# A graph network's finishing stages: bias and shift added on GpSimd, the norm's end writes the new rows, and the norm's root as exp(-0.5 ln)

## What is computed

```python
h = jax.nn.elu(layer_norm(x @ w_in + b_in, g_in, bt_in))
for i in range(L):
    identity = h
    y = gat_conv(h, src, dst, w_l[i], a_s[i], a_d[i], b_l[i])
    y = jax.nn.elu(y)
    y = layer_norm(y, g_l[i], bt_l[i])
    h = y + identity
```

```python
def layer_norm(x, g, b):
    mu = jnp.mean(x, axis=-1, keepdims=True)
    var = jnp.var(x, axis=-1, keepdims=True)
    return (x - mu) * jax.lax.rsqrt(var + EPS) * g + b
```

## Time and profile before

| | us |
|---|---|
| median of 3 runs | 6753.14 |
| lowest, highest | 6741.82, 6756.97 |
| the profiled execution | 6749.72 |
| its span (first to last instruction) | 6747.9 |

### The profile page before, as it was taken

The page is one execution under the profiler, slowest core; times in us unless marked ns, Lnnn a source line. Parts: engine busy times, 40 slices in busy tenths (PEclk is TensorE's granted clock), DMA queues, the critical chain, the costliest instruction groups (busy, mean ns, idle before and its releaser), DMA issues. The chain is left out here.

```text
span 6747.9 us, 97821 instructions
## 1 busy us (share of the span) xinstructions
PE 5290.4 (78%) x22256; PEld 3728.3 (55%) x22256; DVE 4764.2 (71%) x13068; ACT 3945.6 (58%) x13294; POOL 3528.1 (52%) x3571
## 2 busy tenths in 40 slices
PE   1758888845788888458888878999989787777798
PEld 1634445424455555335555547888874566565446
DVE  5756666685677777847777768888871587777793
ACT  4558888874788888648888874444436322111142
POOL 3377777717777776277777740000000577777501
PEclk8878888876899999669999988999999898888899
DMA  6355555435444444454444435555557534333402
GB/s 185 115 151 137 144 140 143 132 103 156 122 124 124 123 128 108 125 144 122 124 126 124 123 82 189 189 190 195 191 189 268 175 117 125 109 108 101 124 2 78
DMA packets 511899, 919.90 MB, mean 136 GB/s; under 512 B 89659, under 2 KB 345611, under 8 KB 511435
## 3 DMA queue, kind: packets, MB, share of 16 engines
q0 software_dynamic: 166320, 446.82, 24.5%
q1 hardware_dynamic: 345259, 469.88, 21.4%
HBM read 773.29 MB, written 152.30 MB: 137 GB/s over the span
## 5 line engine op out<-in xcount | busy, mean ns | idle before, releaser
L1826 POOL DMA_INDIRECT gm_got<-scratch_feat,keep_src_tab x2490 | 2386.6, 958 | 778.5 <-issue 675.0
L2048 ACT ACTIVATE gm_got<-gm_got 128x64 f32<-128x64 f32 x9804 | 2386.6, 337 | 5.3 <-DVE gm_got L1962 5.3
L2104 PE MATMUL gm_bank<-gm_got,gm_onehot 128*128 128x264 f32 x4980 | 1776.2, 455 | 451.0 <-DVE gat_acc L1986 271.9
L2104 PEld LDWEIGHTS gm_bank<-gm_got,gm_onehot 128*128 128x128 f32 x4980 | 881.8, 209 | 1066.6 <-ACT gm_got L2048 691.8
L1986 DVE TENSOR_TENSOR gat_acc<-gat_acc,gm_bank 128x264 f32 x2490 | 1055.7, 424 | 477.1 <-PE gm_bank L2104 198.6
L1114 POOL DMA_INDIRECT mix1a_got<-scratch_rel_feat,layer_rel_tab x240 | 237.9, 991 | 1361.7 <-issue 1360.2
L1114 POOL DMA_INDIRECT mix1b_got<-scratch_rel_feat,layer_rel_tab x590 | 592.9, 1005 | 192.7 <-issue 188.4
L1993 DVE TENSOR_TENSOR gm_onehot<-gm_iota,keep_dst_tab 128x640 f32<-128x640 f32 x498 | 405.5, 814 | 184.8 <-PE gm_bank L2104 181.8
L1171 PE MATMUL mix1b_m_bank<-mix1b_got,mix1b_onehot 128*128 128x256 f32 x1180 | 382.0, 460 | 154.5 <-DVE logit_acc L1145 133.2
L837 POOL DMA_INDIRECT scratch_first<-gat_scores,keep_first_pos x150 | 216.4, 1443 | 486.6 <-DVE gat_scores L820 445.1
L1171 PEld LDWEIGHTS mix1b_m_bank<-mix1b_got,mix1b_onehot 128*128 128x128 f32 x1180 | 243.9, 224 | 259.9 <-DVE mix1b_onehot L1123 151.5
(11 more groups left out here) (578 smaller groups left out, 9538.3 us busy)
## 6 DMA issues: line engine op xcount, KB each, us to landing
moe_w<-scratch_ffn_cut SPq DMA_DIRECT2D x312, 512.0 KB, 3.3
scratch_rel_feat<-rel_out SPq DMA_DIRECT2D x50, 1024.0 KB, 5.2
gm_got<-scratch_feat,keep_src_tab POOLq DMA_INDIRECT x2490, 2.8
gm_flags<-scratch_flags SPq DMA_DIRECT2D x84, 300.0 KB
scratch_feat<-gf_row SPq DMA_DIRECT2D x50, 260.0 KB, 4.1
gm_x<-scratch_x SPq DMA_DIRECT2D x50, 256.0 KB, 3.3
gf_feat<-scratch_feat SPq DMA_DIRECT2D x50, 256.0 KB, 3.9
gf_old<-scratch_hidden SPq DMA_DIRECT2D x50, 256.0 KB, 5.0
```

The costliest lines, as they stand in the source:

```text
L1826: nc.gpsimd.indirect_dma_start(out=got[:, place // GROUPS, place % GROUPS * GROUP + j, 0:GAT_ROW], out_offset=None, in_=dram["feat"][layer ...
L2048: last = nc.scalar.activation(rows, rows, ACT.Copy, scale=got[:, b, i, D + h:D + h + 1])
L2104: nc.tensor.matmul(bank[i % BANKS][:, 0:GAT_SUM], onehot[:, i % HOTS, :], got[:, v[1] % B, i, :], start=True, stop=True).then_inc(s_sum, 1)
```

## The change

1. In `gat_finish` POOL gets two kinds of additions, one instruction of 128 x 512 for each pair: the bias on the own rows, as soon as ACT has scaled them, and the norm's shift on the old rows, as soon as they have landed. DVE's bias pass (L2253) goes.
2. The norm's end on DVE reads the shifted old rows as its second tensor and writes h. DVE's pass L2248 goes.
3. In `GroupNorm`, hence in the input stage too, the root is Ln and then Exp with scale -0.5, both on ACT, and gives 1/sqrt at once. DVE's reciprocal goes. A table that has Ln and Exp is loaded at the stage's start.
4. DVE's wait for the three weight vectors moves from ahead of its first sums to ahead of its first centre; POOL waits for them at its start.

```diff
@@ GroupNorm
     def roots(self, nc, g):
         u, n, size = self.span(g)
         nc.scalar.wait_ge(self.s_mv, n)
-        nc.scalar.activation(self.std[:, u, :], self.mv[:, u, :, 1], ACT.Sqrt, bias=self.eps[:, 0:1]).then_inc(self.s_std, size)
-
-    def invert(self, nc, g):
+        nc.scalar.activation(self.std[:, u, :], self.mv[:, u, :, 1], ACT.Ln, bias=self.eps[:, 0:1]).then_inc(self.s_std, size)
+        nc.scalar.wait_ge(self.s_std, n)
+        nc.scalar.activation(self.rstd[:, u, :], self.std[:, u, :], ACT.Exp, scale=-0.5).then_inc(self.s_rstd, size)
+
+    def inverted(self, nc, g):
         u, n, size = self.span(g)
-        nc.vector.wait_ge(self.s_std, n)
-        nc.vector.reciprocal(self.rstd[:, u, :], self.std[:, u, :]).then_inc(self.s_rstd, size)
         nc.vector.wait_ge(self.s_rstd, n)
@@ gnn_input, ACT (and the same line at the start of ACT in gat_finish)
+                nc.scalar.preload_act_table_set("natural_log_exp_and_others")
                 flow(part, ACT_BODY)
@@ gat_finish, POOL
-                flow(lambda name, g: project.scatter_pool(pool, g), [("scores", 0)])
+                pool.wait_ge(s_w, 48)
+
+                def part(name, g):
+                    if name == "scores":
+                        project.scatter_pool(pool, g)
+                        return
+                    for p in pairs_of(g):
+                        if name == "bias":
+                            pool.wait_ge(s_scaled, p + 1)
+                            nc.gpsimd.tensor_tensor(feat[:, p % DEEP], feat[:, p % DEEP], both(rows["b_l"][:, :]), ALU.add).then_inc(s_biased, 1)
+                        else:
+                            pool.wait_ge(s_old[p % DEEP], landed(p))
+                            nc.gpsimd.tensor_tensor(old[:, p % DEEP], old[:, p % DEEP], both(rows["bt_l"][:, :]), ALU.add).then_inc(s_shifted, 1)
+
+                flow(part, [("bias", 3), ("shift", 2), ("scores", 0)])
@@ gat_finish, DVE
-                dve.wait_ge(s_w, 48)
...
-                            ln.finish(nc, p, yp, rows["bt_l"]).then_inc(s_ya, 1)
+                            dve.wait_ge(ln.s_centred, p + 1)
+                            dve.wait_ge(s_shifted, p + 1)
+                            if p >= UNROLL:
+                                dve.wait_ge(s_sent[u], reuse(p))
+                                dve.wait_ge(project.s_ht, p + 1 - UNROLL)
+                            for i in range(PAIR):
+                                last = nc.vector.scalar_tensor_tensor(h[:, u, i, :], yp[:, i, :], ln.rstd[:, u, i:i + 1], old[:, p % DEEP, i, :],
+                                                                      ALU.mult, ALU.add)
+                            last.then_inc(s_h, 1)
...
-                            dve.wait_ge(s_scaled, p + 1)
+                            dve.wait_ge(s_biased, p + 1)
                             nc.vector.tensor_tensor(yp, yp, feat[:, p % DEEP], ALU.add).then_inc(s_yf, 1)
...
-                            nc.vector.tensor_tensor(h[:, u], old[:, p % DEEP], yp, ALU.add).then_inc(s_h, 1)
+                    if name == "moments" and g == 0:
+                        dve.wait_ge(s_w, 48)
...
-                            nc.vector.tensor_tensor(yp, yp, both(rows["b_l"][:, :]), ALU.add).then_inc(s_yb, 1)
@@ gat_finish, ACT
-                            act.wait_ge(s_yb, p + 1)
+                            act.wait_ge(s_yf, p + 1)
                             elu.part(nc, p, y[:, p % DEEP])
```

More of the change, by code:

```diff
@@ L929, in part @@
                     if name == "scale0":
-                        ln0.invert(nc, g)
+                        ln0.inverted(nc, g)
                     if name == "scale1":
-                        ln1.invert(nc, g)
+                        ln1.inverted(nc, g)
                     for p in pairs_of(g):
@@ L2146, in gat_finish @@
         project = Projection(nc, space, io, dram, keep, gathers, layer + 1, scores, 7)
-        s_w, s_scaled, s_y, s_yf, s_yb, s_elu, s_ya, s_h, s_dve, s_fall, s_factors = (
-            sem(n) for n in ("s_w", "s_scaled", "s_y", "s_yf", "s_yb", "s_elu", "s_ya", "s_h", "s_dve", "s_fall", "s_factors"))
+        s_w, s_scaled, s_biased, s_shifted, s_y, s_yf, s_elu, s_h, s_dve, s_fall, s_factors = (
+            sem(n) for n in ("s_w", "s_scaled", "s_biased", "s_shifted", "s_y", "s_yf", "s_elu", "s_h", "s_dve", "s_fall", "s_factors"))
         s_feat, s_old, s_sent = space.sems("s_feat", DEEP), space.sems("s_old", DEEP), space.sems("s_sent", UNROLL)
@@ L2217, in part @@
                             project.start_dve(dve)
-                        ln.invert(nc, g)
+                        ln.inverted(nc, g)
                     for p in pairs_of(g):
@@ L2241, in part @@
                             ln.aggregate(nc, p)
-                        elif name == "finish":
-                            dve.wait_ge(s_ya, p + 1)
-                            dve.wait_ge(s_old[p % DEEP], landed(p))
-                            if p >= UNROLL:
-                                dve.wait_ge(s_sent[u], reuse(p))
-                                dve.wait_ge(project.s_ht, p + 1 - UNROLL)
-                            nc.vector.tensor_tensor(h[:, u], old[:, p % DEEP], yp, ALU.add).then_inc(s_h, 1)
+                    if name == "moments" and g == 0:
+                        dve.wait_ge(s_w, 48)
                     for p in pairs_of(g):
                         yp = y[:, p % DEEP]
-                        if name == "sums":
-                            dve.wait_ge(s_yf, p + 1)
-                            nc.vector.tensor_tensor(yp, yp, both(rows["b_l"][:, :]), ALU.add).then_inc(s_yb, 1)
-                        elif name == "moments":
+                        if name == "moments":
                             ln.centre(nc, p, yp, yp, rows["g_l"])
```

## The result

The changed kernel takes 6784.9 us (median of 7 runs, 6767.0 to 6793.5), the kernel before 6753.1. Their ratio is 1.0044, with a 95% interval of 1.0034 to 1.0053: slower by about 30 us. The profiled execution took 6767.0 us, span 6765.1, and was the fastest of the seven.

A forecast was written before the change was run, and what follows sets the result against it. Finishing stages were taken as a chain through DVE, PE and ACT, ending on POOL's scatters. Two stages at +10 us less 2.5 in the input stage gave +17.5: 6767 profiled, 6771 median; range 6760 to 6795, 8-in-10 range 6724 to 6798.

The forecast's parts named there:

- What bounded the kernel, and the end on POOL's queue: Finishing stages: POOL owes 89.1 us after group 3's bias, plus 19 us stalls; last scatter 9 us later; +10 taken.
- Two-sided sharing: Finishing stages: POOL additions also shut out DVE, about 1.1 us each with two SBUF operands, 6.5 us a full group.
- The place of that price: DVE's price per full group in finishing stages: 2.2 us in the centre, 1.3 in the sums, 3.0 at the norm's end.
- No gain up to the first projection: Finishing stages: 7.7 us earlier without POOL's cost, but DVE pays 6.5 a group against 6.2 removed, so gains nothing.
- The weights' wait behind the scaling: Finishing stage start: the 3.60 us wait for weights moves to POOL and disappears behind ACT's scaling.
- The roots: Finishing stages: each root ahead of L787 saves 1.0 us, before the first projection and in four later loops: 5.0 us.
- The input stage: Only roots change there: 1.2 us saved at its start and 1.3 near its end, 2.5 us in all.
- The additions disturb nobody: Rival for finishing stages: gains all kept, 13 us a stage, 28 us in all with the input stage, 6725; chance 0.25.
- One-sided: Rival: DVE shuts POOL out, POOL never stops DVE; -3 to +4 us a finishing stage, 6745 to 6758; chance 0.20.
- POOL only in gaps of DVE: Rival: DVE's centre and norm-end passes shut out POOL additions too; about +28 us a finishing stage, 6805; chance 0.10.

The follow-up runs named there:

- the tiny additions: Changed kernel with 24 idle ACT instructions, POOL's bias and shift additions cut to 2 of 256 columns: 6717.1 us, ratio 0.9946 to the kernel before.
- the scatters first: Changed kernel, later loops placed as before, POOL's order turned to scatters, then bias, then shift: 6821.4 us, ratio 1.0081 to the kernel before.
- the shift alone on POOL: Kernel before with changed roots and only the shift added by POOL, bias on DVE, later loops placed as before: 6782.7 us, ratio 1.0026.
- the loops placed: Kernel before with only the roots changed, idle instructions putting later loops at their old places modulo 128: 6760.9 us, ratio 0.9993 on the third chip.
- the roots alone: Kernel before with only the roots changed (Ln, Exp on ACT, no reciprocal), plus 24 idle ACT instructions: 6751.1 us, ratio 0.9998.

## Why the prediction was right, and where it was not

**What bounded the kernel, and the end on POOL's queue: right.** I had 89.1 us of POOL's work owed from the end of group 3's bias, and 19 us of stalls, which put the last scatter 9 us later than before, or up to 17 with feedback. That bias ended at 2850.15, 92.0 us into the stage where I had 88.8, and the last scatter at 2952.85: 102.7 us, so 13.6 of stalls. Counted from the stage's start the last scatter ended 6.5 us later than before. I took +10 us a stage; the stages grew by 4.7 and 6.5. The mechanism held, and the stalls were sized too high.

**Two-sided sharing: right, and its size nearly.** DVE's busy time rose by 7.5 us although 32.3 us of passes went (bias and last addition 15.5 each, six reciprocals of 0.22), so the additions cost it 39.8 us a stage, and the tiny additions give 38.5 by another way. I had 6.5 us a full group, 32 us for 25 pairs, and 1.1 us where an addition meets two SBUF operands; it is 0.77 us over all of them. The Trainium skill (SBUF — State Buffer, Who interferes with whom) calls the port pair that DVE and GpSimd share an exclusive lock, and says that the order of issue decides who blocks. In the centre the trace agrees: an instruction of at most 1.49 us (0.44 to 0.48 undisturbed) is as if it had waited for one POOL addition, and no more. But a DVE addition of 5.31 us at 2906.64, and the one of 11.42 us with the scatters first, outlast several POOL additions in a row, though with the shift alone on POOL the two engines' additions took turns. What decides between turns and a whole run no experiment here shows.

**The place of that price: wrong.** The step put 3.0 us a group at the norm's end, 2.2 in the centre and 1.3 in the sums. The norm's end paid nothing (4.03 to 4.05), the centre 5.1 to 6.8 a group, and the sums 14 us in the stage, where 1.3 a full group makes some 6. I had let DVE run on and the shift wait behind the last bias until the norm's end. The rows show the bias of a group end and its shift begin at once (2790.17, 2818.58) while DVE is in the centre, which started earlier than I had it against ACT's scaling or was held up itself; the whole queue of additions drains there. The row of a scatter of 1.28 us beside L725, from which I took that the centre lets POOL in, told nothing of what POOL does to the centre.

**No gain up to the first projection: right.** Scores of group 0 are copied 79.3 us into the stage, before 77.9, so nothing was gained and 1.4 us lost. Group 0's bias gained 1.2 us (L859 at 19.03 instead of 20.25 us) where I had 1.5.

**The weights' wait behind the scaling: right**, shown by the kernel in which only that wait moves.

**The roots: right in sign on the chain, not in size, and wrong at the end.** I had 5.0 us a stage. Alone they brought the last scores 9.5 us earlier, with the granted clock at 0.73 instead of 0.70 and PE busy for 93.4 us instead of 97.9; what the clock has in that is not separated. But the stage ended only 3.6 us earlier, with more time in the scatters (91.1 us busy, before 84.1), and with the loops placed it ended 2.9 us later than before (97.6 us busy). The step that took a gain on the chain as a gain of the stage left out that POOL's stalls move with DVE.

**The input stage: right.** It is 1.9 to 4.0 us shorter in the profiles of the eight kernels of the table that have the new roots; I had 2.5.

**The rivals.** "The additions disturb nobody" falls with the centre's 9 to 11 us. That rival had -13 us a stage; the tiny additions, which disturb next to nobody but also take next to no time on POOL, give -20. "One-sided" falls with L725 and L2238. "POOL only in gaps of DVE" falls as well: POOL's additions take 1.33 (bias) and 1.44 us (shift) in the median and run beside the centre, alternating with it.

**What I left out.** The change made the kernel about 30 us slower, and the finishing and input stages hold only 8 of that by the profiled execution. The sum took it that stages whose code is untouched keep their time. ACT's loop in the second message stage costs about 12 us, shown from both sides. The first message stage is 4 to 9 us longer than before in all six kernels of the table whose POOL has additions in the finishing stages, and at most 1.5 us longer in the three others. It comes before any addition on POOL has run, and with the tiny additions too, so it is not the sharing. There each of the 830 gathers takes some 7 ns more, at the median (ns, min/median/max; first before, then changed):

```profile
L1826 POOL DMA_INDIRECT gm_got<-scratch_feat,keep_src_tab x830: 940/946/1762, 328.0 to 1379.4; - x166
```

```profile
L1827 POOL DMA_INDIRECT gm_got<-scratch_feat,keep_src_tab x830: 949/953/2394, 325.0 to 1380.7; - x166
```

830 times 7 ns is 5.8 us. In the second message stage of the changed kernel the same row says 946 again. I have no experiment on the cause, so it stays open. Together: 12 + 6 + 11 - 3 = 26 of 30 us; the rest is within the intervals. The predicted 6771 was 14 us short, and it is this omission that made it so: without the two effects in untouched stages, the same sum would have been above what was measured. That it came this near is partly luck: the finishing stages were priced 9 us too high (+20, measured +11), and 18 us elsewhere were not in the sum at all.

No version here that adds the whole bias and shift beats the kernel before by more than can be measured: the roots alone are at 0.9998, and 0.9993 with the loops placed; with the bias on POOL as well the ratio is 0.9987 (0.9970 to 1.0004), on the chip with the wide intervals.

## What to carry over

Before work is moved from DVE to GpSimd, look at what DVE runs at that time: if its passes read two tensors from SBUF, an addition of 1.24 us on the other engine costs DVE some 0.8 us here, more than the 0.62 us a pair that its removed pass had cost. A gain on a chain counts for the stage only if the queue that ends the stage gets shorter too. And for effects under half a per cent, compare the loops' gaps for issue and the code packets in stages that were not edited: fifteen instructions more, even idle ones, cost about 12 us here, as much as the change cost in its own two finishing stages (11).

## What was unexpected of the hardware

- A loop of 273 ACT instructions, moved by 15, gets a gap of 1.5 to 2.4 us in nearly each turn (20.8 us in 16 gaps, 23.1 in 15), with code packets of 8 KB going from 46 to 102; the kernel loses about 12 us. Moved on by 24 more, the gaps are gone. On DVE four gaps of up to 3.9 us cost nothing visible.
- Ten POOL additions in a row beside DVE additions went in two ways. With the scatters first POOL kept its 1.23 us each, and the first of DVE's five took 11.42 us, the five 13.8 instead of 3.1. With the shift alone on POOL the engines took turns: 1.61 us a POOL addition, 1.75 a DVE one.
- A single scatter can stand still for 16.3 us, once for 20.0, beside chains of DVE additions; in the changed kernel, without the bias pass and the last addition on DVE, the longest took 4.7 us.
- Gathers of the first message stage take 953 to 957 ns instead of 946 to 949 in every kernel whose POOL adds in the finishing stages, and 946 to 949 in the message stages after that.
